# The order of SyncE's loads in a fused mLSTM and mixture-of-experts kernel: the max rows two groups ahead, the result's store last

## The chip, the cores and the metric

The kernel runs on one core of one Trainium2 chip. The metric is the device time of a launch in microseconds (us), lower is better. A core has TensorE for matmuls (PE in the profile), VectorE (DVE), ScalarE (ACT), GpSimd (POOL), and SyncE (SP), which here does nothing but issue DMA transfers; each engine works through its own instructions in order, and they wait for each other on semaphores. A wait stops everything that stands behind it on the same engine.

## The reference, cut to what matters

One block of a network on x of shape (8, 1024, 128) in fp32: a matrix LSTM mixer, a layer norm, a mixture of 16 experts of which 4 are chosen per token, and a second layer norm.

```python
# mixer, per batch row and head (4 heads of 64)
x_act  = swish(conv4(x @ W_up[:, :256]));  z = x @ W_up[:, 256:]
q, k   = headwise(x_act, Wq), headwise(x_act, Wk);  v = headwise(x @ W_up[:, :256], Wv)
logD   = cumulated log forget gates + input gates, lower triangle
mD     = max(logD, axis=-1)                       # "the max rows" of the kernel
C      = (q k^T / 8) * exp(logD - mD)
h      = C / (max(|sum C|, exp(-mD)) + 1e-6) @ v
x      = layernorm(x + ((headnorm(h) * norm_w + skip * x_act) * swish(z)) @ W_down)
# experts
g      = sigmoid(x @ gate_w.T);  top 4 of 16, weights divided by their sum -> combine
out    = layernorm(x + sum_e combine_e * (silu(x Win_e) * (x Vin_e)) Wout_e + shared expert)
```

## The kernel before, in words

Phase 1 (up to about 125 us of the span) projects x, runs the convolution and stores x_act and swish(z) to DRAM scratch; a short scan then makes the max rows mD and the decays of all tokens and stores them too. Phase 2 works through 16 groups of 512 tokens, numbered 0 to 15, in order, since a state is carried from one group to the next. All that this text is about lies in phase 2.

In phase 2 every engine runs the same skeleton, `groups` (line 318): `mix(0, None)`, then a hardware loop over g = 1 to 14 with `mix(g, g - 1)`, then `mix(15, 14)`, then the experts of group 15 alone. `mix(g, f)` does the mixer of group g and, woven into it, the experts of group f = g - 1. Each group has four chunks of 128 tokens. Every chunk k makes new values on TensorE, and VectorE adds them to the decayed state: `state<-kept,bank`, line 952, which needs `kept`, the decayed state, from GpSimd, line 569. I call these four additions S0 to S3.

GpSimd's order in `mix(g, f)` is written out by hand: kept 0, the skip product of the first half (`mixed`, line 575), kept 1, skip product of the second half, then `args(g + 1, 0)`, kept 2, `args(g + 1, 1)`, kept 3. `args(g + 1, kp)` makes logD - mD of the next group for two of its chunks: two subtractions `D<-a_tok,max_b` (line 540) and two maskings (line 550). The subtractions read `max_b`, a tile of 128 x 2048 that holds the next group's max rows on every partition. It is loaded from DRAM by SyncE (`load_max`, line 405), and there is one such tile, so the load for group g + 2 may start only when the last subtraction for group g + 1 is done. Each subtraction adds 1 to the semaphore `arg_sub`, four for each group.

VectorE's order around that place is: S0, parts of the routing of group f, an expert product, S1, then a chain of five small instructions on 128 x 64 tiles that splits the combine weights into three bf16 parts (lines 1085 to 1093, the "comb chain"), the score products C (line 935), the key product (line 941), two expert products, S2. TensorE transposes the result of the comb chain (line 1382) ahead of the third slot of the experts' matmuls. `y<-bank,x_res` (line 1009) is the sum of mixer and residual late in a group; I call its start y1.

SyncE's order before is in `mix` (line 456): wait for all four subtractions for group g, load the max rows of g + 1, then xT, inter_w, xa and silu_z of g + 1, each behind the wait for its tile to come free, then the store of the result of group g - 1, then the residual x_res.

Of the kernel before, what the change touches and what calls it, by code (L numbers as in the profile page):

```python
# [43 lines left out]
def mixer_moe_block(nc, x, W_up, conv_w, conv_b, Wq, Wk, Wv, W_ig, b_ig, W_fg, b_fg, norm_w, skip,  # L44
# [7 lines left out]
    HALO = TAPS - 1  # L52
    NP = INNER // P
    NX, _, HX = e_win.shape
    NJ = NX * HX // P
    TOPK = 4
# [3 lines left out]
    NG = B * HALVES  # L60
# [5 lines left out]
    x_g = x.rearrange("b (f k p) e -> (b f) p k e", f=HALVES, p=P)  # L66
# [7 lines left out]
    with ExitStack() as ctx:  # L74
        def sb(name, shape, dt=F32):
            return ctx.enter_context(nc.sbuf_tensor(name, shape, dt))

        def sem(name):
            return ctx.enter_context(nc.semaphore(name))
# [148 lines left out]
        x_res = sb("x_res", [P, NC, E])  # L228
# [42 lines left out]
        xa_in, xT_in, x_res_in = sem("xa_in"), sem("xT_in"), sem("x_res_in")  # L271
# [6 lines left out]
        arg_sub = sem("arg_sub")  # L278
# [16 lines left out]
        y1_done, st1_done, mv1_done, ve1_done = sem("y1_done"), sem("st1_done"), sem("mv1_done"), sem("ve1_done")  # L295
# [16 lines left out]
        def nth(g, per, i):  # L312

            return g * per + i + 1
# [5 lines left out]
        def groups(eng, mix, ffn):  # L320


            mix(0, None)
            with eng.Fori(1, NG - 1) as g:
                mix(g, g - 1)
            mix(NG - 1, NG - 2)
            ffn(NG - 1)

        def prev(eng, s, g, per=1):

            if isinstance(g, int) and g == 0:
                return
            eng.wait_ge(s, g * per)
# [8 lines left out]
        def _(sp):  # L342
            n = [0]
# [60 lines left out]
            def load_max(g):  # L404
                sp.dma_start(max_b[:], max_d[g].rearrange("h t -> (h t)").partition_broadcast(P)).then_inc(max_in, 16)

            def load_inter(g):
                for par in range(2):
                    sp.dma_start(inter_w[par * DH:(par + 1) * DH],
                                 inter_d[g].rearrange("(p two) t -> two p t", two=2)[par].partition_broadcast(DH)  # L410
                                 ).then_inc(inter_in, 16)

            def load_xa(g):
                sp.dma_start(xa[:], xact_d[g].rearrange("p (s t) -> p s t", t=G)[:, 0:NP]).then_inc(xa_in, 16)
# [4 lines left out]
            def load_z(g):  # L419
                sp.dma_start(silu_z[:], xact_d[g].rearrange("p (s t) -> p s t", t=G)[:, NP:]).then_inc(z_in, 16)  # L420
# [30 lines left out]
            sp.wait_ge(rows_stored, 16 * (HALVES * NC + 1))  # L451

            def mix(g, f):
                sp.wait_ge(arg_sub, nth(g, 4, 3))
                if not (isinstance(g, int) and g == NG - 1):
                    load_max(g + 1)
                    sp.wait_ge(val_mm[1], g + 1)
                    sp.dma_start(xT2[:], xt_d[g + 1]).then_inc(xT_in, 16)
                    sp.wait_ge(qs_done, g + 1)
                    load_inter(g + 1)  # L460

                    sp.wait_ge(skip_done, nth(g, NP, NP - 1))
                    sp.wait_ge(score_mm[1][1], g + 1)
                    load_xa(g + 1)
                    for p in range(NP):
                        sp.wait_ge(hs_done[p], g + 1)
                    load_z(g + 1)
                if f is not None:
                    store(f)
                if not (isinstance(g, int) and g == NG - 1):  # L470
                    sp.wait_ge(y1_done, g + 1)
                    sp.dma_start(x_res[:], x_g[g + 1]).then_inc(x_res_in, 16)

            def store(f):
                sp.wait_ge(out_done, f + 1)
                sp.dma_start(out_g[f], out_sb[:]).then_inc(out_stored, 16)

            groups(sp, mix, store)
            sp.wait_ge(out_stored, 16 * NG)


        @block.gpsimd
        def _(pool):
# [129 lines left out]
            pool.wait_ge(decay_in, 16 * 2 * NP)  # L613
            pool.wait_ge(phase2_const, 5)
            groups(pool, mix, ffn)


        @block.scalar
        def _(act):
# [179 lines left out]

            decays(0)  # L800
            groups(act, mix, ffn)


# [731 lines left out]
```

## Time and profile before

| | us |
|---|---|
| median of 3 runs | 912.57 (912.12 to 923.52) |
| the profiled execution | 916.93 |
| its span, first to last instruction | 915.2 |
| TensorE busy in the span | 823.2 (90%) |
| VectorE busy | 669.4 (73%) |
| GpSimd busy | 372.1 (41%) |
| ScalarE busy | 363.3 (40%) |
| DMA, mean of the span | 89 GB/s |

The span is the profile's; the time of the execution is 1.7 us longer for what lies around it. Busy time of an engine is no measure of what bounds the kernel in one place; for that the chain of waits and the timeline of one group are read. All times inside the span are from its start.

### The profile page before, as it was taken

The page shows a single profiled execution, that of the slowest core. Times are in us where ns is not written, and L with a number is a line of the kernel's source. Part 1 is how long each engine was busy: PE and PEld are TensorE (multiplying, and loading weights), DVE is VectorE, ACT ScalarE, POOL GpSimd, SP SyncE. Part 2 cuts the span into 40 slices and gives each one's busy share as a digit, 9 for nine tenths or more (in the row PEclk, how much of TensorE's full clock was granted, in tenths as well). Part 3 has the DMA queues.
Part 4 walks back from the last instruction along what each step waited for, and adds up shares of the span by engine and source line. Part 5 has one row for each costly group of instructions (what it writes and reads, how often), then busy time and mean ns, then how long its engine had stood idle before and what let it go on. Part 6 is the DMA issues. An engine that isn't in the chain of part 4 may idle for free.

```text
span 915.2 us, 17726 instructions
## 1 busy us (share of the span) xinstructions
PE 823.2 (90%) x5783; PEld 643.9 (70%) x5783; DVE 669.4 (73%) x1759; ACT 363.3 (40%) x621; POOL 372.1 (41%) x372
## 2 busy tenths in 40 slices
PE   6879866799999999899989999999999999999966
PEld 5646655677777777777777777777777777777754
DVE  5899944577777777777786878777867777878654
ACT  4767742224343434333333443333434343433131
POOL 5040037253536262626262626353726353534200
PEclk8999977699999999999999999999999999999979
DMA  4877734300403040404030403040304040400000
GB/s 114 258 242 271 272 116 119 115 25 24 126 23 126 24 126 23 126 23 126 23 126 23 126 23 126 23 126 23 126 23 126 23 126 23 126 23 24 1 11 12
DMA packets 53104, 81.01 MB, mean 89 GB/s; under 512 B 10176, under 2 KB 36952, under 8 KB 49112
## 3 DMA queue, kind: packets, MB, share of 16 engines
q1 hardware_dynamic: 53080, 80.68, 28.2%
q8 instruction: 16, 0.26, 0.1%
q14 instruction: 8, 0.07, 0.0%
HBM read 55.24 MB, written 25.43 MB: 88 GB/s over the span
## 4 chain that ended last, share of the span: by engine, by line
PE 49%; DVE 17%; issue 14%; DMA 10%; POOL 5%; SPq 3%; ACT 2%; POOLq 1%; DVEq 0%; ACTq 0%
PE bank L1402 12%; DMA max_b<-max_scratch 7%; PE bank L1372 5%; PE bank L1376 5%; PE bank L1373 5%; PE bank L1392 4%; PE bank L1345 3%; DVE st L991 3%; PE bank L1321 3%; DVE acc L839 2%; PE bank L1319 2%; DVE Y L1003 2%; PE bank L1326 2%; DMA x_in<-in_L_attn_x_dram 2%; DVE out_sb L1003 2%
## 5 line engine op out<-in xcount | busy, mean ns | idle before, releaser
L755 ACT ACTIVATE s_in<-bank 128x512 f32<-128x512 f32 x144 | 85.9, 597 | 195.9 <-PE bank L1376 195.0
L1402 PE MATMUL bank<-ewout,h 128*128 128x128 f32 x1024 | 146.5, 286 | 0.0
L1402 PEld LDWEIGHTS bank<-ewout,h 128*128 128x128 f32 x1024 | 123.9, 191 | 25.4 <-issue 25.4
L554 POOL TENSOR_TENSOR rs<-ve,half 128x4 f32<-128x4 f32 x32 | 32.6, 1019 | 267.5 <-DVE ve L999 267.5
L1103 DVE TENSOR_TENSOR h<-s_in,bank 128x512 f32<-128x512 f32 x144 | 98.1, 681 | 58.5 <-PE bank L1376 50.3
L1372 PE MATMUL bank<-yT_hi,in_hi 128*128 128x512 f32 x288 | 128.2, 445 | 6.8 <-DVE h L1103 6.8
L1376 PE MATMUL bank<-yT_lo,in_hi 128*128 128x512 f32 x288 | 115.3, 400 | 0.0
L1373 PE MATMUL bank<-yT_hi,in_lo 128*128 128x512 f32 x288 | 114.6, 398 | 0.0
L540 POOL TENSOR_TENSOR D<-a_tok,max_b 128x512 f32<-128x512 f32 x64 | 65.4, 1043 | 118.5 <-DVE max_b L911 67.9
L1107 DVE TENSOR_TENSOR h<-h,bank 128x512 f32<-128x512 f32 x128 | 87.3, 682 | 19.8 <-PE bank L1392 19.8
L952 DVE TENSOR_TENSOR state<-kept,bank 64x130 f32<-64x130 f32 x128 | 36.6, 286 | 64.8 <-POOL kept L569 34.7
L621 ACT ACTIVATE u_sb<-bank 128x260 f32<-128x260 f32 x64 | 24.8, 387 | 148.9 <-PE bank L1321 148.9
L1321 PE MATMUL bank<-vals,C 128*128 128x65 f32 x512 | 73.0, 266 | 0.0
L1319 PE MATMUL bank<-state,qs 128*128 128x130 f32 x256 | 55.9, 301 | 17.4 <-issue 15.1
L582 POOL TENSOR_TENSOR r_h<-var_h,half 128x8 f32<-128x8 f32 x32 | 52.9, 1653 | 42.9 <-DVE var_h L972 41.8
L1321 PEld LDWEIGHTS bank<-vals,C 128*128 128x128 f32 x512 | 69.4, 197 | 0.0
L1372 PEld LDWEIGHTS bank<-yT_hi,in_hi 128*128 128x128 f32 x288 | 55.5, 193 | 18.8 <-DVE h L1103 12.9
L839 DVE SCALAR_TENSOR_TENSOR acc<-xm,vecs,acc 128x512 f32<-128x512 f32 x96 | 68.2, 780 | 0.0
L569 POOL TENSOR_TENSOR kept<-state,decay 128x260 f32<-128x260 f32 x64 | 39.7, 620 | 70.1 <-DVE state L952 69.9
L1376 PEld LDWEIGHTS bank<-yT_lo,in_hi 128*128 128x128 f32 x288 | 55.1, 191 | 12.7
L1373 PEld LDWEIGHTS bank<-yT_hi,in_lo 128*128 128x128 f32 x288 | 55.7, 193 | 5.4
L1319 PEld LDWEIGHTS bank<-state,qs 128*128 128x128 f32 x256 | 41.0, 196 | 26.1 <-issue 23.8
(197 smaller groups left out, 1634.2 us busy)
## 6 DMA issues: line engine op xcount, KB each, us to landing
xact_scratch<-xact SPq DMA_DIRECT2D x16, 1024.0 KB, 4.9
max_b<-max_scratch SPq DMA_DIRECT2D x15, 1024.0 KB, 7.7
xa<-xact_scratch SPq DMA_DIRECT2D x16, 512.0 KB, 6.4
silu_z<-xact_scratch SPq DMA_DIRECT2D x16, 512.0 KB, 3.8
inter_w<-inter_scratch SPq DMA_DIRECT2D x30, 256.0 KB, 7.0
x_in<-in_L_attn_x_dram SPq DMA_DIRECT2D x16, 256.0 KB, 4.9
xt_scratch<-x_t SPq DMA_DIRECT2D x16, 256.0 KB, 4.8
xT<-xt_scratch SPq DMA_DIRECT2D x16, 256.0 KB, 8.0
```

Of the source, the lines that this page charges most:

```text
L540: pool.tensor_tensor(D[:, kp, par], a_g.rearrange("p k (s two) -> p two k s", two=2)[:, par, 2 * kp:2 * kp + 2] .unsqueeze(3).to_broadcast ...
L582: pool.tensor_tensor(r_h[:, c].rearrange("p k h -> p (k h)"), var_h[:, c].rearrange("p k h -> p (k h)"), half[:, 0:2 * NH], ALU.pow).then_ ...
L755: act.activation(s_in[:, j % 2], bank[4][:], ACT.Silu).then_inc(silu_done, 1)
L839: i = dve.scalar_tensor_tensor(a, src, vecs[:, p, t:t + 1], a, ALU.mult, ALU.add)
L1103: dve.tensor_tensor(dst[:, j % 2], s_in[:, j % 2], bank[5][:], ALU.mult).then_inc(h1_done, 1)
L1107: dve.tensor_tensor(h2[:, (j - 1) % 2], h1[:, (j - 1) % 2], bank[6][:], ALU.mult).then_inc(h2_done, 1)
L1319: pe.matmul(o, qs[:, p, c], state[:, p], start=True, stop=False, skip_group_check=True)
L1321: i = pe.matmul(o[:, par * DV:(par + 1) * DV], C[:, par, kk, p], vals[:, k, 2 * p + par], start=False, stop=True, skip_group_check=True)
L1372: pe.matmul(o, in_hi[:, m, j], yT_hi[:], start=True, stop=False)
L1373: pe.matmul(o, in_lo[:, m, j], yT_hi[:], start=False, stop=False)
L1376: pe.matmul(o, in_hi[:, m, j], yT_lo[:], start=False, stop=True).then_inc(done, 1)
L1402: i = pe.matmul(bank[7][:, k * P:(k + 1) * P], h2[:, j % 2, k * P:(k + 1) * P], w, start=(j == k == 0), stop=(j == NJ), skip_group_check=True)
```

## The change: what it does

SyncE's list in `mix(g, f)` is put in another order. The load of the max rows is taken from the head of the list to behind the load of xa and is now for group g + 2: it waits for the four subtractions for group g + 1, that is for the end of the reading of the tile. The residual load comes ahead of the store of the result, which is now last. The load for group 1 is issued once ahead of the groups. Because a load two groups ahead is absent in the last two groups, `groups` has groups 1 and 14 written out beside the loop on every engine, and the loop runs from 2 to 13. The instructions of the other four engines and their order within a group are the same.

```diff
--- before.py
+++ after.py
@@ -321,10 +321,15 @@
 
 
             mix(0, None)
-            with eng.Fori(1, NG - 1) as g:
+            mix(1, 0)
+            with eng.Fori(2, NG - 2) as g:
                 mix(g, g - 1)
+            mix(NG - 2, NG - 3)
             mix(NG - 1, NG - 2)
             ffn(NG - 1)
+
+        def is_last(g, n=1):
+            return isinstance(g, int) and g >= NG - n
 
         def prev(eng, s, g, per=1):
 
@@ -451,9 +456,7 @@
             sp.wait_ge(rows_stored, 16 * (HALVES * NC + 1))
 
             def mix(g, f):
-                sp.wait_ge(arg_sub, nth(g, 4, 3))
-                if not (isinstance(g, int) and g == NG - 1):
-                    load_max(g + 1)
+                if not is_last(g):
                     sp.wait_ge(val_mm[1], g + 1)
                     sp.dma_start(xT2[:], xt_d[g + 1]).then_inc(xT_in, 16)
                     sp.wait_ge(qs_done, g + 1)
@@ -462,19 +465,24 @@
                     sp.wait_ge(skip_done, nth(g, NP, NP - 1))
                     sp.wait_ge(score_mm[1][1], g + 1)
                     load_xa(g + 1)
+                if not is_last(g, 2):
+                    sp.wait_ge(arg_sub, nth(g + 1, 4, 3))
+                    load_max(g + 2)
+                if not is_last(g):
                     for p in range(NP):
                         sp.wait_ge(hs_done[p], g + 1)
                     load_z(g + 1)
+                    sp.wait_ge(y1_done, g + 1)
+                    sp.dma_start(x_res[:], x_g[g + 1]).then_inc(x_res_in, 16)
                 if f is not None:
                     store(f)
-                if not (isinstance(g, int) and g == NG - 1):
-                    sp.wait_ge(y1_done, g + 1)
-                    sp.dma_start(x_res[:], x_g[g + 1]).then_inc(x_res_in, 16)
 
             def store(f):
                 sp.wait_ge(out_done, f + 1)
                 sp.dma_start(out_g[f], out_sb[:]).then_inc(out_stored, 16)
 
+            sp.wait_ge(arg_sub, 4)
+            load_max(1)
             groups(sp, mix, store)
             sp.wait_ge(out_stored, 16 * NG)
```

SyncE in the loop, the head of the list before (`L405` the max rows; rows marked ISA are waits with computed values):

```order
L405 ISA [waits arg_sub]
L405 DMA max_b<-max_scratch 128x2048
L458 ISA [waits val_mm_1]
L458 DMA xT<-xt_scratch 128x512
L409 DMA inter_w<-inter_scratch 64x2x512 [waits qs_done]
L409 ISA
L409 DMA inter_w<-inter_scratch 64x2x512
L462 ISA
L414 ISA [waits score_mm_1_1,skip_done]
L414 DMA xa<-xact_scratch 128x1024
```

and of the change (`L410` the max rows):

```order
L461 ISA [waits val_mm_1]
L461 DMA xT<-xt_scratch 128x512
L414 ISA [waits qs_done]
L414 DMA inter_w<-inter_scratch 64x2x512
L414 ISA
L414 DMA inter_w<-inter_scratch 64x2x512
L465 ISA
L419 ISA [waits score_mm_1_1,skip_done]
L419 DMA xa<-xact_scratch 128x1024
L469 ISA
L410 ISA [waits arg_sub]
L410 DMA max_b<-max_scratch 128x2048
```

The max load has moved from the head of the list, ahead of xT, to behind xa.

SyncE in the loop, the end of the list before (`L476` the store, `L472` the residual):

```order
L420 ISA [waits hs_done_1,hs_done_0]
L420 DMA silu_z<-xact_scratch 128x1024
L476 ISA [waits out_done]
L476 DMA out_dram<-out_sb 128x4x128
L472 DMA x_res<-in_L_attn_x_dram 128x4x128 [waits y1_done]
```

and of the change (`L482` the store, `L476` the residual):

```order
L425 ISA [waits hs_done_1,hs_done_0]
L425 DMA silu_z<-xact_scratch 128x1024
L476 DMA x_res<-in_L_attn_x_dram 128x4x128 [waits y1_done]
L482 ISA [waits out_done]
L482 DMA out_dram<-out_sb 128x4x128
```

The store of the result has changed places with the residual load and is now the last row of a group.

## Rows read from the trace of the kernel before

**Rows 1.** The page: the granted clock in 40 slices, and the chain by line.
```profile
PEclk8999977699999999999999999999999999999979
...
PE bank L1402 12%; DMA max_b<-max_scratch 7%; PE bank L1372 5%; PE bank L1376 5%; PE bank L1373 5%; PE bank L1392 4%; PE bank L1345 3%; DVE st L991 3%; PE bank L1321 3%; DVE acc L839 2%; PE bank L1319 2%; DVE Y L1003 2%; PE bank L1326 2%; DMA x_in<-in_L_attn_x_dram 2%; DVE out_sb L1003 2%
```

**Rows 2.** The list of waits: engine, line, for whom; total us, times, longest.
```profile
POOL D L540 <- DMA max_b<-max_scratch: 49.6, 14, 5.5
```

**Rows 3.** Tile max_b: SyncE's issue in group 6, and its loads' time to land.
```profile
417.98 0.35 SPq L405 DMA_DIRECT2D max_b<-max_scratch  x1
...
DMA to landing us min/median/max: 4.8/7.7/9.3
```

**Rows 4.** Timeline of group 6, GpSimd, then VectorE: start, duration, instruction, idle before.
```profile
420.35 1.63 POOL L575 TENSOR_SCALAR mixed<-xa,vecs 128x512 f32<-128x512 f32 x1
...
427.21 2.04 POOL L540 TENSOR_TENSOR D<-a_tok,max_b 128x512 f32<-128x512 f32 x2 [5.24 <-DMA max_b<-max_scratch]
...
421.73 0.59 DVE L952 TENSOR_TENSOR state<-kept,bank 64x130 f32<-64x130 f32 x2 [0.46 <-PE bank L1326]
...
423.33 0.20 DVE L1093 CAST comb<-comb_r 128x64 bf16<-128x64 f32 x1
...
431.12 0.59 DVE L952 TENSOR_TENSOR state<-kept,bank 64x130 f32<-64x130 f32 x2 [4.31 <-POOL kept L569]
```

**Rows 5.** Timeline of group 1, GpSimd, then VectorE; the max rows were there already.
```profile
188.20 2.04 POOL L540 TENSOR_TENSOR D<-a_tok,max_b 128x512 f32<-128x512 f32 x2
...
191.40 0.61 POOL L569 TENSOR_TENSOR kept<-state,decay 128x260 f32<-128x260 f32 x1
...
188.41 0.59 DVE L952 TENSOR_TENSOR state<-kept,bank 64x130 f32<-64x130 f32 x2 [0.89 <-PE bank L1326]
...
189.32 0.99 DVE L1087 TENSOR_TENSOR comb_r<-comb 128x64 f32<-128x64 f32 x1
...
191.53 0.53 DVE L1093 CAST comb<-comb_r 128x64 bf16<-128x64 f32 x1
...
197.20 0.59 DVE L952 TENSOR_TENSOR state<-kept,bank 64x130 f32<-64x130 f32 x2 [1.84 <-PE bank L1326]
```

**Rows 6.** Timeline of group 7, GpSimd, then VectorE.
```profile
470.11 2.04 POOL L540 TENSOR_TENSOR D<-a_tok,max_b 128x512 f32<-128x512 f32 x2 [0.97 <-DMA max_b<-max_scratch]
...
468.89 0.59 DVE L952 TENSOR_TENSOR state<-kept,bank 64x130 f32<-64x130 f32 x2 [0.46 <-PE bank L1326]
...
471.27 0.94 DVE L1093 CAST comb<-comb_r 128x64 bf16<-128x64 f32 x1
```

**Rows 7.** Timeline of group 8: GpSimd, VectorE, and the group's y1.
```profile
518.82 2.04 POOL L540 TENSOR_TENSOR D<-a_tok,max_b 128x512 f32<-128x512 f32 x2 [2.96 <-DMA max_b<-max_scratch]
...
515.62 0.59 DVE L952 TENSOR_TENSOR state<-kept,bank 64x130 f32<-64x130 f32 x2 [0.46 <-PE bank L1326]
...
545.16 0.69 DVE L1009 TENSOR_TENSOR y<-bank,x_res 128x512 f32<-128x512 f32 x1 [1.29 <-PE bank L1345]
```

**Rows 8.** Timeline of VectorE: y1 of groups 1, 6, 7 and 14.
```profile
219.83 0.69 DVE L1009 TENSOR_TENSOR y<-bank,x_res 128x512 f32<-128x512 f32 x1 [1.29 <-PE bank L1345]
...
453.22 0.69 DVE L1009 TENSOR_TENSOR y<-bank,x_res 128x512 f32<-128x512 f32 x1 [1.29 <-PE bank L1345]
...
499.97 0.69 DVE L1009 TENSOR_TENSOR y<-bank,x_res 128x512 f32<-128x512 f32 x1 [1.29 <-PE bank L1345]
...
821.94 0.69 DVE L1009 TENSOR_TENSOR y<-bank,x_res 128x512 f32<-128x512 f32 x1 [1.29 <-PE bank L1345]
```

**Rows 9.** Timeline of TensorE: three instructions after long gaps, and one later.
```profile
66.91 0.50 PE L1210 MATMUL bank<-x_lo,up_hi 128*128 128x512 f32 x1 [2.45 <-DVE x_lo L816]
...
192.12 0.40 PE L1382 MATMUL bank<-ident_bf,comb 128*128 128x128 bf16 x4 [2.07 <-DVE comb L1093]
...
884.08 0.61 PE L1382 MATMUL bank<-ident_bf,comb 128*128 128x128 bf16 x4 [2.94 <-DVE comb L1093]
...
886.73 0.55 PE L1376 MATMUL bank<-yT_lo,in_hi 128*128 128x512 f32 x1
```

## The prediction

> **What bounds the kernel now.** I read the page first. TensorE is busy through phase 2 at full clock (the 9s of [rows 1] from the ninth slice to the 38th; a slice is 22.9 us), and the chain by line is made of its matmuls with one foreign entry, the DMA of the max rows with 7%. The list of waits says what that is: GpSimd waits for the load 14 times, 49.6 us in all [rows 2]. Then the timeline of one group, 6, shows whom that holds up. SyncE issues the load at 417.98, behind the last group's store, and a load takes 4.8 to 9.3 us to land [rows 3]. GpSimd ends the second skip product at 420.35 + 1.63 = 421.98, stands for 5.24 us and starts the subtractions at 427.21; kept 2 is queued behind them, so S2 starts at 431.12 after 4.31 us of waiting [rows 4]. This is a real stall on the path. The groups run in a ring, so I measure it by the ring's period: y1 goes from 219.83 (group 1) to 821.94 (group 14), 13 periods in 602.11 us, 46.32 us each [rows 8].
>
> The whole stall is not a loss, though, and this is what the reader is to see next. In group 8 the load lands earlier (wait 2.96), and from S1 at 515.62 to y1 at 545.16 it takes 29.54 us [rows 7]. In group 6, with a wait of 5.24, it takes 453.22 - 421.73 = 31.49 [rows 4, 8]. But in group 7 the load was there almost at once (wait 0.97), and the same stretch takes 499.97 - 468.89 = 31.08 [rows 6, 8]; in group 1 it did not wait at all, and it takes 219.83 - 188.41 = 31.42 [rows 5, 8]. The earliest max rows give stretches nearly as slow as the latest. The reason stands in the rows between: with the subtractions beside them, instructions of the comb chain take 0.99 and 0.53 us [rows 5] and 0.94 us [rows 6], where the same cast takes 0.20 us without [rows 4]. Each of the long ones ends just after a GpSimd instruction ends: line 1087 in group 1 at 190.31, the second subtraction at 190.24; line 1093 at 192.06, kept 2 at 192.01 [rows 5]. So VectorE gets through once between two GpSimd instructions. TensorE waits for the chain's end: 2.07 us in group 1 [rows 9].
>
> **The change part by part.**
>
> *The max load.* It is issued when the subtractions for the next group end, around 430 in the time of group 6, and at most 9.3 us later it has landed [rows 3], far ahead of its use one period later. The wait of GpSimd goes from all of groups 2 to 14, 13 in number; group 0's load keeps its place, and group 1 had no wait. That alone removes every stall like that of group 6.
>
> *What is late next.* Nothing else holds GpSimd, so in each of the 13 groups the subtractions start when the second skip product ends: 421.98 in the time of group 6, which is S1 + 0.25 [rows 4]. This is the position of group 1 (D at 188.20, S1 at 188.41), not of group 8 (D 3.20 us after S1). From group 1 I take what follows. The comb chain ends at 191.53 + 0.53 = 192.06, that is D + 3.86: five VectorE instructions have let two subtractions, two maskings and kept 2 pass. S2 starts at 197.20, 5.14 after the chain's end; y1 at 219.83 is 22.63 after S2, so y1 is the chain's end + 27.77 [rows 5, 8]. Group 7 checks it: chain end 472.21, y1 at 499.97, 27.76 [rows 6, 8]. Then S1 to y1 is 0.25 + 3.86 + 27.77 = 31.88 us. From y1 to the next S1 it is 468.89 - 453.22 = 15.67, and 15.65 from 499.97 to 515.62 [rows 6 to 8]; nothing in that piece is touched. The period is 31.88 + 15.67 = 47.55 us, against 46.32 now: 1.23 us more, and 13 times that is 16.0 us.
>
> Bounds for this term: below, only two of the five instructions meet GpSimd, as in group 7, whose whole period is 499.97 - 453.22 = 46.75, which makes 13 x 0.43 = 5.6 us. Above, each of the five meets a whole subtraction at 0.99 us, so the chain takes about 5.0 us where I have S1 + 4.11 less the 0.6 of S1 itself, 3.5: 1.5 us more a group, another 19.5 us. I take the value from group 1, since it has the same five against five in the same order; the upper end needs five subtractions in a row, and GpSimd has two. The trace has only this one group with the start so early.
>
> The Trainium skill, "SBUF — State Buffer", section on who interferes with whom, says that VectorE and GpSimd share a port pair as an exclusive lock held for a whole instruction, and that casts, and tensor_tensor with both inputs in SBUF, can need it. It gives no price. The trace agrees by the 0.94 against 0.20 us of the cast. By the rule alone the earlier load would be no gain, and by the naive reading of the list of waits it would be one of up to 49.6 us.
>
> *The other loads.* xT, inter_w, xa and silu_z keep their waits and order; they land sooner without the 1 MB load ahead of them, and no engine waits for them now (the only DMA in the chain's leading lines inside a group is the max load [rows 1]), so it is worth nothing. silu_z stands behind the new wait on `arg_sub`, which ends near 430, while its own tile comes free only late in the group, where the second half of `mixed` is done: no cost. The residual load and the store change places; the residual is used a period later. If a store were late VectorE would wait with its output a period on; there is room of tens of us. Price 0 for all, with 0.5 us either way.
>
> The same page says DMA never contends with a compute engine. No row here tests that for the new place of the max load, and the sum has 0 for it anyway.
>
> *The written-out groups.* The instructions executed are the same; the jump into the loop comes one group later. The last group, already written out, has no row that shows a price; I put 0, within 1 us.
>
> **Sum.** 916.93 + 16.0 = 932.9 us in the measure of the profiled execution. That execution is 4.4 us above the median of 912.57. If this is luck of the loads' landing, the changed kernel doesn't share it, since its subtractions no longer depend on the landing: 932.9 stands. If it is a cost of profiling, the median will be 928.5. I can't tell them apart and predict the middle, **931 us**.
>
> **The rivals.**
>
> 1. *Faster: the wait goes and the chain gets through.* If the comb chain is past before GpSimd begins, every group is like group 8: 29.54 + 15.67 = 45.21, 1.11 less than now, 13 times: -14.4 us, 902.5, or 898 by the median. It decides at the start of the subtractions: they must come 3 us after S1 as in [rows 7], and by the order on GpSimd they come 0.25 us after. It could still hold if the slow comb chain of group 1 belonged to that group alone; group 7 speaks against it. Chance 0.07.
> 2. *Partly.* The locking is as light as in group 7 or lighter, 0 to 5.6 us more: 913 to 922. For it: one group only shows the full case. Chance 0.12.
> 3. *TensorE's clock.* TensorE would wait some 2.5 us for the comb chain in each group (0.25 + 3.86 against the 3.65 of group 1, 0.46 on top of its 2.07). After gaps of 2.07 and 2.45 us the clock stayed full, after one of 2.94 it fell to half: four transposes took 0.61 us where they take 0.40, and the 39th slice, in which this lies, has a 7 (granted 0.7 to 0.8 of 2.4 GHz, a mean of 2.4 and 1.2) [rows 1, 9]. My gap lies between. The spell at half clock went from 884.08 to the last slow row at 886.73 [rows 9], 2.65 us, in which half as much is done: 1.3 us lost. 13 times that is 17 us: 950. For some groups only, 934 to 950. Chance 0.08.
> 4. *No effect:* the load is as late as before, because SyncE is held at `arg_sub` by something. Nothing stands between it and the tile's last reader. 912 to 917; chance 0.03.
>
> **How the numbers follow.** The forecast has 0.70, its own range 927 to 935. With 2% of 912.57 as about what a measurement of this kernel can tell from no change, slower by over 2% begins at 930.8, in the middle of my forecast: 0.38 of the 0.70 lies above, 0.32 below. With rival 3, slower is 0.46; with rivals 2, 4 and most of 1, same is 0.52; faster by over 2% needs 894, below even rival 1, and gets 0.02. The range goes from 918, which takes in half of rival 2 and the light half of the lower bound, to 942, with the milder part of rival 3; it leaves out the rest of rivals 1 to 4, under 0.2.
>
> **What would show it.** Right: no wait of GpSimd on the max load from group 2 on; each comb chain some 3.5 us long and TensorE waiting about 2.5 us at line 1382 (in the changed file a few lines on); periods all alike at 47.5; VectorE no longer waiting for kept 2. Wrong: comb instructions of 0.2 us beside the subtractions, or periods under 46.3, or matmul spacing of 0.43 us in mid-group.

## The result and the profile after

The changed kernel takes 940.71 us (937.25 to 943.35, 4 runs) against 918.01 us for the kernel before (912.12 to 923.52, now 4 runs): a ratio of 1.0246, 95% interval 1.0148 to 1.0344. A second comparison gave 939.55 against 917.11, ratio 1.0236 [1.0186, 1.0286]. So it is slower, by some 2.4%; both intervals lie wholly above 1, and both reach below 1.02, so that the loss is over 2% is likely and not certain. 931 us was forecast, with 918 to 942 as the range.

The page of the changed kernel: its span, the granted clock in 40 slices and the chain by line.

```profile
span 941.4 us, 17502 instructions
...
PEclk8789978699999999999999999999999999999979
...
PE bank L1410 14%; PE bank L1380 7%; PE bank L1384 7%; PE bank L1381 7%; PE bank L1329 5%; PE bank L1400 4%; PE bank L1327 4%; PE bank L1334 4%; DVE acc L847 3%; PE bank L1353 3%; DVE st L999 3%; PE bank L1368 2%; DVE Y L1011 2%; DVE comb_r L1095 2%; PE bank L1343 1%
```

The max load, which had 7% of the chain [rows 1], is gone from it. The clock row has 9s through phase 2 as before; a spell of under 3 us at the lower level does not show in slices of 23.5 us and has to be looked for in TensorE's rows, below.

Tile max_b: what its readers waited for (total us, times), and the loads' time to land. The line on VectorE's C belongs to the second subtractions, which wait for D to be read; the wait on the load is down from 49.6 us [rows 2] to 1.6, once, in group 0.

```profile
  DVE C L943: 13.1, 14
...
  DMA max_b<-max_scratch: 1.6, 1
...
DMA to landing us min/median/max: 4.5/4.7/6.8
```

SyncE in group 6 (start, duration, instruction): the store at 427.77, xT next, the max load only at 440.22, behind the four subtractions for group 7.

```profile
427.77 0.41 SPq L482 DMA_DIRECT2D out_dram<-out_sb  x1
...
428.70 0.35 SPq L461 DMA_DIRECT2D xT<-xt_scratch  x1
...
440.22 0.33 SPq L410 DMA_DIRECT2D max_b<-max_scratch  x1
```

GpSimd in group 6: the second skip product ends at 433.27 and the subtractions start at once, without an idle time.

```profile
431.64 1.63 POOL L583 TENSOR_SCALAR mixed<-xa,vecs 128x512 f32<-128x512 f32 x1
...
433.24 2.04 POOL L548 TENSOR_TENSOR D<-a_tok,max_b 128x512 f32<-128x512 f32 x2
...
435.24 1.22 POOL L558 TENSOR_SCALAR_AFFINE_SELECT D<-D 128x512 f32<-128x512 f32 x2
...
436.43 0.62 POOL L577 TENSOR_TENSOR kept<-state,decay 128x260 f32<-128x260 f32 x1
```

VectorE in the same stretch. These lines answer to [rows 4] and [rows 5]:

```profile
433.02 0.59 DVE L960 TENSOR_TENSOR state<-kept,bank 64x130 f32<-64x130 f32 x2 [0.47 <-PE bank L1334]
...
433.64 0.69 DVE L1093 CAST comb<-comb 128x64 bf16<-128x64 f32 x1
...
434.36 0.99 DVE L1095 TENSOR_TENSOR comb_r<-comb 128x64 f32<-128x64 f32 x1
...
435.39 0.53 DVE L1097 CAST comb<-comb_r 128x64 bf16<-128x64 f32 x1
...
435.95 0.58 DVE L1099 TENSOR_TENSOR comb_r<-comb_r,comb 128x64 f32<-128x64 f32 x1
...
436.57 0.53 DVE L1101 CAST comb<-comb_r 128x64 bf16<-128x64 f32 x1
...
437.13 1.29 DVE L943 TENSOR_TENSOR C<-bank,D 128x512 f32<-128x512 f32 x2
...
442.23 0.59 DVE L960 TENSOR_TENSOR state<-kept,bank 64x130 f32<-64x130 f32 x2 [1.84 <-PE bank L1334]
```

Lay the two lists side by side. S1 is at 433.02, the first subtraction at 433.24, 0.22 after it. The first cast starts at 433.64 and ends at 434.33, just after the first subtraction (433.24 + 1.02 = 434.26); the next ends at 435.35, just after the second (435.28); the third and fourth follow the two maskings; the fifth ends at 437.10, just after kept 2 (437.05). The chain takes 3.46 us and ends 4.08 us after S1; S2 starts at 442.23, 5.13 after that. Nothing waits for `kept` any more.

y1 of groups 1, 6 and 14:

```profile
225.29 0.69 DVE L1017 TENSOR_TENSOR y<-bank,x_res 128x512 f32<-128x512 f32 x1 [1.23 <-PE bank L1353]
...
464.85 0.69 DVE L1017 TENSOR_TENSOR y<-bank,x_res 128x512 f32<-128x512 f32 x1 [1.29 <-PE bank L1353]
...
847.78 0.69 DVE L1017 TENSOR_TENSOR y<-bank,x_res 128x512 f32<-128x512 f32 x1 [1.22 <-PE bank L1353]
```

TensorE's transposes behind the comb chain in group 6 and in group 7:

```profile
437.15 0.40 PE L1390 MATMUL bank<-ident_bf,comb 128*128 128x128 bf16 x4 [2.49 <-DVE comb L1101]
...
484.71 0.61 PE L1390 MATMUL bank<-ident_bf,comb 128*128 128x128 bf16 x4 [2.50 <-DVE comb L1101]
```

The gap is 2.5 us in both, against 0.2 where the chain is undisturbed. In group 7 the four transposes take 0.61 us instead of 0.40. The granted clock of that stretch is half (start and end of the stretch, its length; the number behind POOL's is the clock):

```profile
484.70:487.50 2.80, 2.79 (x10) 2.17 (x10) 1.87 (x3) 1.19 (x2) 1.95 (x2) 0.50 0.06 23
```

TensorE's clock has fallen to its lower level, 1.2 GHz, and is back at 2.4 from 487.5 on; S1 to y1 is 33.11 us there instead of 31.84. The same happened in groups 2 and 13 and in no other of the 13.

The sum by pieces. From y1 of group 1 to y1 of group 14 it was 602.11 us [rows 8] and is now 622.49: 20.4 us more, with a period of 47.5 to 47.8 in the ten groups without the clock's fall and of 48.8 to 49.1 in the three with it. 13 x 1.23 is 16.0, and three falls are 4.1. The rest of the difference of the spans, 26.2 us, lies mostly ahead of the groups. S0 of group 0 in the trace before

```profile
142.53 0.59 DVE L952 TENSOR_TENSOR state<-kept,bank 64x130 f32<-64x130 f32 x2 [2.80 <-PE bank L1326]
```

and after:

```profile
146.98 0.59 DVE L960 TENSOR_TENSOR state<-kept,bank 64x130 f32<-64x130 f32 x2 [1.76 <-PE bank L1334]
```

is 4.45 us later. Phase 1 is the same in both kernels. The granted clock was lower in it this time: 0.77 from 23 to 46 us where the trace before has 0.99, and 0.90 against 0.98 from 46 to 69. In the other traces of this study S0 of group 0 lies anywhere from 139.7 to 145.1 whatever the kernel, and at 142.64 in the second trace of the changed kernel itself, so I take this as chance. The other 1.4 us are in groups 0 and 1 and behind group 14.

### The profile page after: what moved, and what is told of

The parts are those of the page before. It is cut to its first block, busy times and chain, and to the rows that moved or that the text cites. A ratio compares the mean times of both kernels' runs of the same rounds, so it can differ in the third digit from the quotient of the medians.

```text
span 941.4 us, 17502 instructions
## 1 busy us (share of the span) xinstructions
PE 830.7 (88%) x5783; PEld 651.9 (69%) x5783; DVE 686.2 (73%) x1759; ACT 345.7 (37%) x607; POOL 371.5 (39%) x372
## 4 chain that ended last, share of the span: by engine, by line
PE 63%; DVE 20%; issue 11%; ACT 2%; POOL 2%; DMA 2%; SPq 1%; DVEq 0%; POOLq 0%; ACTq 0%
PE bank L1410 14%; PE bank L1380 7%; PE bank L1384 7%; PE bank L1381 7%; PE bank L1329 5%; PE bank L1400 4%; PE bank L1327 4%; PE bank L1334 4%; DVE acc L847 3%; PE bank L1353 3%; DVE st L999 3%; PE bank L1368 2%; DVE Y L1011 2%; DVE comb_r L1095 2%; PE bank L1343 1%
```

## Experiments

**Theory A**: the time is set by when GpSimd's subtractions start. While a GpSimd instruction runs, a comb-chain instruction of VectorE can't go; the chain's end sets S2 and y1 until the subtractions come so late that kept 2 does. **Rivals**: B, the groups written out; C, the new places of loads and store; D, chance in the first comparison. Where "wait for the chain" is said, GpSimd has one more wait ahead of the first subtractions, on the counter of VectorE's routing steps.

**The changed kernel again.** Edit: none.

> The changed kernel itself once more. Theory A: 13 periods of 47.55 us, except those in which TensorE's clock falls after its gap of 2.5 us (1.3 us each): time 935 to 945, and 15 to 25 us above the kernel before on the same chip. If the comparison made so far was luck of the loads' landing (rival): within 10 us of before.

Measured: 939.55 (938.01 to 941.57), before 917.11. Ten periods of 47.55 us or close to it, and three at 48.9 to 49.1, in groups 2, 8 and 14 this time. The kernel before ran beside it on the same chip. Rival D is out.

**Only the groups written out.**

```diff
             mix(0, None)
-            with eng.Fori(1, NG - 1) as g:
+            mix(1, 0)
+            with eng.Fori(2, NG - 2) as g:
                 mix(g, g - 1)
+            mix(NG - 2, NG - 3)
             mix(NG - 1, NG - 2)
```

> Only the groups 1 and 14 written out beside the loop, SyncE's order as before. Theory A (the loss is VectorE's comb chain behind GpSimd's subtractions, which start 0.22 us after S1): the subtractions still start when the late load lands, so the periods scatter between 45.2 and 47.4 us as before, mean near 46.3, time 912 to 924. Theory B (the written-out groups and the later jump into the loop cost the time): period or entry grows, 930 to 941.

Measured: 919.16, before 920.48, ratio 0.9993 [0.9946, 1.004]. The periods scatter from 45.7 to 47.2. Rival B is out: this part costs nothing that the times can tell. The traces do show a little. From y1 to the next S1 it takes 15.71 to 15.75 us in the loop of every kernel with groups 1 and 14 written out, and 15.64 to 15.67 in every one without, and 0.3 us more or, in two traces, 0.8 once, ahead of group 3. That is about 1 to 2 us in all; why is open.

**The groups written out and the end of SyncE's list changed, the max load at its head as before.**

```diff
                     load_z(g + 1)
-                if f is not None:
-                    store(f)
-                if not (isinstance(g, int) and g == NG - 1):
                     sp.wait_ge(y1_done, g + 1)
                     sp.dma_start(x_res[:], x_g[g + 1]).then_inc(x_res_in, 16)
+                if f is not None:
+                    store(f)
```

> The kernel before with the groups written out and only the tail of SyncE's list changed: residual load ahead of the store, max load at the head as before. All theories that blame the max load's place: no difference, periods scatter 45.2 to 47.4 with the landing, 912 to 924. If the store's place mattered: VectorE would wait before out_sb or the periods would all be longer than in the kernel before.

Measured: 939.86 and 953.16 in two runs, before 914.8, ratio 1.04 [1.02, 1.06]. Both lie far above my 912 to 924, and of all the misses this one taught most. SyncE in group 7 of this kernel, and the loads' time to land:

```profile
472.74 0.41 SPq L477 DMA_DIRECT2D out_dram<-out_sb  x1
...
473.69 0.35 SPq L407 DMA_DIRECT2D max_b<-max_scratch  x1
...
DMA to landing us min/median/max: 4.4/4.8/5.7
```

The max load is now issued 0.95 us after the store's issue; before, the residual load stood between and it was 1.5 us. And the residual load, 256 KB, is no longer in flight with it: before, it was issued 1.0 us ahead of the max load and landed 2.1 us after that one's issue, and now it has landed 8 us earlier. The max load lands in 4.8 us at the median where it took 7.7 [rows 3]. The store, 256 KB too, is just ahead of it in both, so it is not any transfer ahead that does this; by what way the residual load does it no run shows. Before, three of the 13 loads landed in under 5.1 us beside it all the same (groups 3, 7 and 11). So the max rows are a few microseconds earlier, and GpSimd starts 0.3 to 1.6 us after S1 where it was 1.2 to 5.7; in group 7, 0.60 us after it:

```profile
478.59 2.04 POOL L541 TENSOR_TENSOR D<-a_tok,max_b 128x512 f32<-128x512 f32 x2 [0.35 <-DMA max_b<-max_scratch]
```

```profile
477.99 0.59 DVE L953 TENSOR_TENSOR state<-kept,bank 64x130 f32<-64x130 f32 x2 [0.46 <-PE bank L1327]
...
478.61 1.07 DVE L1086 CAST comb<-comb 128x64 bf16<-128x64 f32 x1
...
481.93 0.53 DVE L1094 CAST comb<-comb_r 128x64 bf16<-128x64 f32 x1
```

The chain (first and last row) ends 4.47 us after S1, later than in the changed kernel. The mean period of groups 2 to 14 is 48.10 us, and five groups (2, 4, 5, 11 and 12) have a spell at the lower clock, behind gaps of TensorE of 2.1 to 2.8 us. The load is not two groups ahead here, and yet the whole loss is there. That is theory A in its strongest form: what costs is that the max rows are early, not how they come to be early. Rival C is right only in that the place of the residual load matters, through the landing of the max load.

**The changed kernel with GpSimd waiting for the chain.**

```diff
                     if k in (1, 2) and not (isinstance(g, int) and g == NG - 1):
+                        if k == 1 and f is not None:
+                            pool.wait_ge(route, f * ROUTE + 14)
                         args(g + 1, k - 1)
```

> The changed kernel, and GpSimd waits for the end of the comb chain before the next group's subtractions. Theory A: the chain is 1.2 us long again, ends 1.8 us after S1, S1 to y1 is 29.5 us, the period 45.2 in all 13 groups against 47.88 on average: span 941.4 - 35 = 906.6, time about 908. TensorE's gap before line 1390 is 0.2 us and there are no spells at half clock in groups 2 to 14. Theory C (the max load in its new place beside xa, or the new order on SyncE, slows the groups): the period stays above 47, time 935 or more.

Measured: 904.27 (902.16 to 904.8), before 920.48, ratio 0.9855 [0.9764, 0.9945]; once more beside another experiment, 903.73 against 921.41, 0.9813 [0.9756, 0.9871]. GpSimd, then VectorE, in group 6:

```profile
418.57 2.05 POOL L548 TENSOR_TENSOR D<-a_tok,max_b 128x512 f32<-128x512 f32 x2 [1.88 <-DVE comb L1103]
```

```profile
416.44 0.59 DVE L962 TENSOR_TENSOR state<-kept,bank 64x130 f32<-64x130 f32 x2 [0.46 <-PE bank L1336]
...
417.06 0.20 DVE L1095 CAST comb<-comb 128x64 bf16<-128x64 f32 x1
...
418.04 0.20 DVE L1103 CAST comb<-comb_r 128x64 bf16<-128x64 f32 x1
...
423.37 0.59 DVE L962 TENSOR_TENSOR state<-kept,bank 64x130 f32<-64x130 f32 x2 [1.84 <-PE bank L1336]
```

All subtractions wait 1.9 us and the chain's rows are at 0.20 again; the mean period of groups 2 to 14 is 45.31, TensorE's gap 0.2 us, and no group has the lower clock. The same loads, in the same places, and 36 us less than the changed kernel (35.8 on one chip). The subtractions now run beside the score products C, and these take 0.69 and 0.68 us as without them: of VectorE's work here it is the chain that is hurt. What was expected of the repeat:

> The changed kernel with GpSimd waiting for the comb chain, on the same chip as the run beside it: 902 to 905 and periods of 45.3, 10 to 17 us under the kernel before. Rival (the gain seen was the chip's or the day's): within 5 us of the kernel before.

**The kernel before with the same wait.** The same edit on the kernel before.

> The kernel before, with the same wait of GpSimd for the comb chain, loads in the old order. Theory A: groups whose load landed early (3, 7 and 11 in the trace of before) fall to a period of 45.2, gaining 0.7 to 1.5 us each; late ones keep their stall. In all 1 to 4 us less than before, 909 to 920. Rival (a wait on GpSimd there is itself the gain, whatever the load does): about 908, like the changed kernel with the wait.

Measured: 914.81, before 920.48, ratio 0.9963 [0.992, 1.0005]. One group whose load was early falls to 45.22; the others keep starts of 3.7 to 5.2 us after S1 and periods of 45.4 to 46.9. So the stall that the change takes away was real, about 10 us between this kernel and the one above, and the change needs the wait to have it. The rival is out: the wait by itself, on the old loads, gives 0.8% at most.

**Doses: a wait for three, and for two, of the five chain instructions** (`+ 12` and `+ 11` in place of `+ 14`).

> The changed kernel, and GpSimd waits for three of the five instructions of the comb chain, so that the subtractions start about 1.3 us after S1. Theory A: the last one or two are held up by a subtraction, the chain ends 2.5 to 3.3 us after S1 as in groups 11 and 7 of before, period 46.0 to 46.7, span 917 to 926, time 918 to 928. Rival (only that GpSimd is behind VectorE's S1 matters, the chain does not): the same time as with the full wait, 908.

> The changed kernel with GpSimd waiting for two of the five chain instructions. With three (the run before) the subtractions started 1.65 us after S1 in the loop and missed the chain, but 1.40 after S1 in groups 1 and 14, where one cast was caught: chain end 2.53, S1 to y1 30.3. Theory A: now the groups of the loop start about 1.4 after S1 and all lose that cast, period 46.0 instead of 45.3; groups 1 and 14 start about 1.1 after S1 and lose two, 46.8. Rival (loop and written-out groups differ in something else): the loop stays at 45.3.

Measured for three: 904.94, before 920.48. My number was 918 to 928. The wait itself takes time: from the end of the third instruction, 1.31 us after S1, to the start of the subtraction it is 0.34 us, so the subtractions started 1.65 us after S1 and not 1.3, and met no chain in the loop. The time is thus the one that the rival gave, 908, and can't tell the two theories apart; what does is group 14 of this run and the run with the wait for two. GpSimd and VectorE in group 6, where the last cast has started 0.04 us ahead of the subtraction and passes:

```profile
423.33 1.05 POOL L548 TENSOR_TENSOR D<-a_tok,max_b 128x512 f32<-128x512 f32 x1 [1.40 <-DVE comb_r L1101]
...
423.29 0.20 DVE L1103 CAST comb<-comb_r 128x64 bf16<-128x64 f32 x1
```

and in group 14, where GpSimd is 0.25 us quicker, the fourth instruction just passes and the fifth is caught:

```profile
785.34 2.08 POOL L548 TENSOR_TENSOR D<-a_tok,max_b 128x512 f32<-128x512 f32 x2 [1.23 <-DVE comb L1099]
...
785.29 0.23 DVE L1101 TENSOR_TENSOR comb_r<-comb_r,comb 128x64 f32<-128x64 f32 x1
...
785.55 0.92 DVE L1103 CAST comb<-comb_r 128x64 bf16<-128x64 f32 x1
```

Measured for two: 916.65, before 914.8, 1.0028 [0.9986, 1.0071]. The groups of the loop started at 1.42 and each lost that one cast, period 46.0; groups 1 and 14 started at 1.15 and lost two, 31.0 us from S1 to y1. That is the forecast to 0.1 us. The rival, that loop and written-out groups differ in something else, would have left the loop at 45.3. All doses together give the curve: start at S1 + 0.22, 1.15, 1.42, 1.65, 2.13; S1 to y1 31.84, 31.03, 30.28, 29.56, 29.55.

The trace of the kernel before has the rest of the curve, where the subtractions come late. Start 3.20 us after S1 (group 8) gives 29.54, 3.64 (group 14) 29.65, 4.71 (group 4) 30.72, and the latest, in group 10 with S1 at 606.63, 5.73 and 31.73:

```profile
612.35 2.04 POOL L540 TENSOR_TENSOR D<-a_tok,max_b 128x512 f32<-128x512 f32 x2 [5.48 <-DMA max_b<-max_scratch]
```

```profile
638.35 0.69 DVE L1009 TENSOR_TENSOR y<-bank,x_res 128x512 f32<-128x512 f32 x1 [1.29 <-PE bank L1345]
```

So a start from 1.65 to 3.2 us after S1 costs nothing, an earlier one costs through the chain and a later one through kept 2. In all traces S2 starts 5.13 us after the chain's end or 0.10 us after kept 2's end, whichever is later, the groups with a spell at the lower clock aside.

**GpSimd's first instructions without reading.** Left out: the values of logD - mD; a fill with a constant stands in for each subtraction in groups 1 to 15.

```diff
                     prev(pool, C_done[kp][par], g)
+                    if not (isinstance(g, int) and g == 0):
+                        alone(pool)
+                        pool.memset(D[:, kp, par].rearrange("p k s t -> p (k s t)"), -1.0).then_inc(arg_sub, 1)
+                        continue
                     pool.tensor_tensor(
```

> The changed kernel, in which the subtractions are replaced by fills with a constant (left out: logD - mD of groups 1 to 15), which write SBUF and read nothing; the maskings still read. Theory A1 (a GpSimd instruction holds the comb chain up only if it reads SBUF): chain instructions beside the fills take 0.20 to 0.25 us, those beside the maskings longer. Theory A2 (any GpSimd instruction holds it up): those beside the fills end with the fills.

Measured: 923.05, one run. GpSimd, then VectorE, in group 5:

```profile
374.67 0.99 POOL L550 MEMSET D<- 128x512 f32 x2
...
375.61 1.23 POOL L562 TENSOR_SCALAR_AFFINE_SELECT D<-D 128x512 f32<-128x512 f32 x2
...
375.09 0.61 DVE L1097 CAST comb<-comb 128x64 bf16<-128x64 f32 x1
...
375.74 0.59 DVE L1099 TENSOR_TENSOR comb_r<-comb 128x64 f32<-128x64 f32 x1
...
376.36 0.53 DVE L1101 CAST comb<-comb_r 128x64 bf16<-128x64 f32 x1
```

The two fills take 0.5 us each. The cast starts under the first and ends at 375.70, just after the second (374.67 + 0.99 = 375.66): fills, which read nothing, hold a cast up. By the Trainium skill, "SBUF — State Buffer", on who interferes with whom, a cast can need both halves of the shared pair, and a tensor_tensor with two inputs in SBUF meets only GpSimd's reads; the run shows the first of the two. The tensor_tensor instructions of the chain lie beside a masking and beside kept 2 here, which both read, so for them this run leaves open whether a fill would hold them up. The chain is shorter (end 3.27 us after S1, 4.08 with the subtractions), with fills of 0.5 us against 1.04, though the cast lost its turn between the two fills.

**kept 2 ahead of the subtractions**, on the changed loads and on the old ones; the first subtractions wait for the chain and stand ahead of kept 3, the second behind it.

```diff
+                    if k == 3 and not (isinstance(g, int) and g == NG - 1):
+                        if f is not None:
+                            pool.wait_ge(route, f * ROUTE + 14)
+                        args(g + 1, 0)
                     ...  # kept k, as before
-                    if k in (1, 2) and not (isinstance(g, int) and g == NG - 1):
-                        args(g + 1, k - 1)
+                    if k == 3 and not (isinstance(g, int) and g == NG - 1):
+                        args(g + 1, 1)
```

> The changed loads, and on GpSimd kept 2 goes ahead of the next group's first subtractions, which also wait for the end of the comb chain; the second pair follows kept 3. Theory A: only kept 2 meets the chain, as in group 15 of both traces: chain end 2.1 us after S1, S2 7.2 after S1. S1 to y1 29.9, more by up to 0.9 where the second subtractions meet the head scale: period 45.5 to 46.4, time 906 to 920.

> The kernel before with its old order of loads, and only GpSimd's order changed as in e6. Theory A (the late load costs time only because kept 2 is queued behind the subtractions): S2 is 7.2 us after S1 in every group although the load still lands up to 5.7 us after S1; period 45.5 to 46.4, time 906 to 920, the same as e6. Rival (the late max rows hold the group up by another way as well): periods scatter with the landing as before, mean 46.3 or more, 915 to 922.

Measured: 909.45 with the changed loads, 0.9929 [0.9896, 0.9963], and 908.89 with the old ones, 0.9901 [0.9867, 0.9934], before 917.11. With the old loads in group 6 GpSimd still stands 3.37 us for the load, and it costs nothing, since kept 2 is done:

```profile
419.38 0.62 POOL L573 TENSOR_TENSOR kept<-state,decay 128x260 f32<-128x260 f32 x1 [0.52 <-DVE state L956]
...
423.37 2.04 POOL L540 TENSOR_TENSOR D<-a_tok,max_b 128x512 f32<-128x512 f32 x2 [3.37 <-DMA max_b<-max_scratch]
```

All 13 periods are 45.6 though the start of the subtractions moves between 2.5 and 4.8 us after S1. The rival is out: the late load costs only through what is queued behind it on GpSimd. Both lose 0.4 us a group (45.7 against 45.3, 45.6 against 45.2) against the same loads with the plain wait, since kept 2 meets the chain.

**The kernel before, with the list's end changed and the wait for the chain** (the two edits above; loop and max load as before).

> The kernel before (loop as it was, max load one group ahead at the head of SyncE's list), with the residual load ahead of the store and GpSimd waiting for the comb chain. Theory A: with the residual load out of its way the max load lands 0.3 to 1.6 us after S1, as in the run that changed the tail alone; there it met the chain, here it is waited for, so S1 to y1 is 29.55 and the period 45.2 in all groups, time 901 to 907, as with the two-ahead load and the wait. Rival (only a load two groups ahead takes the stall away): periods scatter to 46 and more as in the run of the kernel before with the wait, 911 to 921.

Measured: 900.78 (900.0 to 904.39), before 921.41, ratio 0.9783 [0.9726, 0.9841]; the changed kernel with the wait, beside it, 903.73. SyncE, GpSimd and the landing:

```profile
411.45 0.41 SPq L475 DMA_DIRECT2D out_dram<-out_sb  x1
...
412.40 0.35 SPq L405 DMA_DIRECT2D max_b<-max_scratch  x1
...
418.84 2.05 POOL L539 TENSOR_TENSOR D<-a_tok,max_b 128x512 f32<-128x512 f32 x2 [1.89 <-DVE comb L1094]
...
DMA to landing us min/median/max: 4.4/5.1/7.4
```

Every period of groups 2 to 14 is 45.2. The load of one group ahead is early enough once the residual load is out of its way, and the wait keeps it from being too early. This beats both kernels. To the changed kernel with the wait the times differ by less than their scatter; its traces are longer by 0.1 us a group, which goes with the written-out groups.

## Why the prediction was right, and where it was off

- *The stall goes, in 13 groups.* Right; the wait is gone from the list.
- *What is late next is the comb chain, and by how much.* Right to 0.05 us: start at S1 + 0.22 (0.25 forecast), chain end 3.86 after it (3.86), S1 to y1 31.84 (31.88), y1 to the next S1 15.72 (15.67), period 47.55 (47.55). That the period fits to the hundredth is luck, of two small errors that cancel. One group of the trace before, group 1, carried all of it, and the wait for the chain takes all of it back.
- *The Trainium skill, "SBUF — State Buffer", who interferes with whom,* gave an exclusive lock for a whole instruction, first come first served. The rows show VectorE's half of it: chain instructions that start under one of GpSimd's end 0.05 to 0.08 us after it, and a cast that starts 0.04 us ahead of a subtraction goes through. That GpSimd is blocked in its turn they hardly show: the subtraction behind that cast took 1.05 us, the one behind a tensor_tensor in group 14 1.08, against 1.04. And with the fills the order was another: the cast's start is 0.04 us ahead of the second fill's, 375.09 against 375.13, and the fill went first, in all 12 groups of that loop.
- *The written-out groups at nothing.* Right within what the times can tell, ratio 0.9993; by the traces it is 1 to 2 us, a little over the 1 allowed.
- *The residual load and the store at nothing.* Right for this change, in whose trace nothing waits for the residual or the store, and wrong as a statement on that edit: it was priced by who uses the residual, and not by what the transfer does to the one issued next. By itself, beside the old max load, it costs at least as much as the whole change (ratio 1.04, two runs).
- *TensorE's clock* was rival 3, with 0.08 for all groups or some. It came in three groups of 13 in each of two traces, behind a gap of 2.4 to 2.5 us, for 1.3 us each: 4 us. Behind the same gap the clock stayed full in the other ten. In other runs it stayed full behind one of 2.88 and fell behind one of 1.68, so the gap's length alone doesn't decide, and setting my gap between 2.45 and 2.94 said nothing. I had the price right and had the chance of a part of it too low.
- *The last step, from the profiled execution to the median*, is the one that was wrong. I took the 4.4 us between 916.93 and 912.57 as half a cost of profiling and predicted 931 in place of the sum's 932.9. The kernel before, run 47 times more beside the experiments, has medians of 914.8 to 921.4, so 912.57 was a lucky median of three. That the landing of its loads moves it fits the runs with kept 2 first, in which the same loads cost nothing and six runs lie within 2.0 us (907.97 to 909.96). The sum's 932.9, with 4 us for the clock, makes 937, at the low end of the runs of 937.25 to 943.35; of the 3.7 and 2.6 us that are left to the two medians, 1.4 are those of groups 0 and 1 and the end in the profiled execution, and the rest stays open.
- *The chances.* I gave 0.52 to no change beyond 2%, 0.46 to slower and 0.02 to faster, so the outcome was not the one I held likeliest, though by little. What I had put too low (the clock, the last step, the written-out groups) all lay on one side, and the time landed 1.3 us inside the upper end of the range.

## What to carry to other kernels

A wait on a load that one engine shows in the list of waits may, as here, be keeping two engines out of each other's way; before it is taken away, look in the trace for a stretch where the load happened to be early, and read the other engine's rows there. Here GpSimd, which had work to place freely, was better held by a wait on the last instruction of the chain that it disturbed than by the chance of a DMA. And the residual load, issued just ahead of the critical one, was part of that one's price, though nobody waited for it.

## What the runs showed of the hardware that was not expected

- Two fills by GpSimd (128 x 512, 0.5 us each), which read nothing from SBUF, stretched a VectorE cast of 0.20 us to 0.61, past the gap between them.
- Beside the subtractions and maskings VectorE gets exactly one chain instruction through between two back-to-back GpSimd instructions, and these are themselves not slowed (subtractions 1.04 us at the median of both traces). Between the two fills it got none.
- A 1 MB load to 128 partitions issued 1.0 us behind the 256 KB residual load took 7.7 us to land at the median (4.8 to 9.3), and 4.8 (4.4 to 5.7) without it, with a 256 KB store just ahead in both.
- GpSimd started 0.34 us after the end of the VectorE instruction that it waited for, in the loop; in the written-out group 14 it was 0.09 us.
- TensorE's clock fell to its lower level in 3 of 13 nearly identical stretches behind gaps of 2.4 to 2.5 us, and in the run with the fills once behind a gap of 1.68; behind one of 2.88 it stayed at 2.4 GHz.
